# Two state sums moved forward in TensorE's program of a fused attention, scan and gated-product kernel

## What is computed

```python
h = x @ fc1_w.T + fc1_b
xz = h @ in_proj_w.T                      # xc, z = split(xz)
u = silu(conv4(xc) + conv_b)
dt_low, Bm, Cm = split(u @ x_proj_w.T)    # 16 states
dt = softplus(dt_low @ dt_proj_w.T + dt_proj_b)
A = -exp(A_log)
def step(h, t):                           # over 2048 positions
    h = exp(dt_t * A) * h + (dt_t * u_t) * B_t
    y_t = einsum('bdn,bn->bd', h, C_t)
out = (((ys + u * D) * silu(z)) @ out_proj_w.T) @ fc2_w.T + fc2_b
ffn = (silu(x @ w_gate.T / 127) * (x @ w_up.T / 127)) @ w_down.T / 127
x = x + out * silu(ffn)
```

## Time and profile before

| | us |
|---|---|
| median of three runs | 2783.31 |
| lowest and highest run | 2783.25, 2787.44 |
| profiled execution, its own time | 2788.2 |
| its span | 2786.4 |
| PE busy | 2542.0 (91%) |
| DVE busy | 2333.8 (84%) |
| ACT busy | 2011.2 (72%) |
| POOL busy | 2013.2 (72%) |

### The profile page before, as it was taken

The page is one execution under the profiler, slowest core; times in us unless marked ns, Lnnn a source line. Parts: engine busy times, 40 slices in busy tenths (PEclk is TensorE's granted clock), DMA queues, the critical chain, the costliest instruction groups (busy, mean ns, idle before and its releaser), DMA issues. The chain is left out here.

```text
span 2786.4 us, 37406 instructions
## 1 busy us (share of the span) xinstructions
PE 2542.0 (91%) x13454; PEld 1490.8 (54%) x13454; DVE 2333.8 (84%) x2899; ACT 2011.2 (72%) x3253; POOL 2013.2 (72%) x682
## 2 busy tenths in 40 slices
PE   7897899999976799999999999999999999999988
PEld 3454344443443465656656566565655656556565
DVE  7685777777733899898998989989899898998996
ACT  4222466666643798897988979889798897988974
POOL 0656011111211999999999999999999999999996
PEclk9898999999978799999999999999999999999999
DMA  6337999888541231321313213132131321313210
GB/s 188 116 116 179 260 218 236 205 200 224 211 161 49 105 130 29 117 92 46 130 26 119 92 46 130 25 120 92 46 130 24 121 92 46 130 24 114 92 46 8
DMA packets 121586, 316.00 MB, mean 113 GB/s; under 512 B 15517, under 2 KB 76445, under 8 KB 104878
## 3 DMA queue, kind: packets, MB, share of 16 engines
q1 hardware_dynamic: 91210, 233.32, 27.3%
q0 software_dynamic: 27888, 79.24, 10.3%
q10 hardware_dynamic: 2304, 1.05, 0.2%
HBM read 278.89 MB, written 43.13 MB: 116 GB/s over the span
## 5 line engine op out<-in xcount | busy, mean ns | idle before, releaser
L1523 DVE TENSOR_TENSOR_SCAN l_st<-l_p_a,l_hl,l_st 128x512 f32<-128x512 f32 x768 | 930.2, 1263 | 90.5 <-ACT l_p_a L1808 83.3
L1721 POOL TENSOR_TENSOR l_st<-l_st,lw_cs 128x2048 f32<-128x2048 f32 x192 | 878.4, 4634 | 3.2 <-ACT l_hl L1813 3.2
L1808 ACT ACTIVATE l_p_a<-l_dt,lw_a_neg 128x512 f32<-128x512 f32 x1024 | 666.5, 681 | 67.2 <-DVE keep_xg L1523 41.1
L1713 POOL TENSOR_TENSOR l_st<-l_bs,l_dtu 128x2048 f32<-128x2048 f32 (+1 forms) x128 | 555.1, 4337 | 57.2 <-PE l_p_y L2098 53.3
L2098 PEld LDWEIGHTS l_p_y<-keep_ident,l_st 128*128 128x128 f32 x3072 | 355.1, 145 | 118.6 <-issue 73.0
L2098 PE MATMUL l_p_y<-keep_ident,l_st 128*128 128x128 f32 x3072 | 380.5, 281 | 28.7 <-POOL l_st L1721 28.7
L1020 ACT ACTIVATE a_pr<-a_p_s 128x512 f32<-128x512 f32 x512 | 284.7, 596 | 143.8 <-PE a_p_s L1089 140.0
L931 DVE TENSOR_REDUCE a_mpart<-a_p_m 128x1 f32<-128x512 f32 x512 | 312.0, 679 | 12.2 <-PE a_p_m L1045 11.0
L1523 DVE TENSOR_TENSOR_SCAN keep_xg<-l_p_a,l_hl,keep_xg 128x512 f32<-128x512 f32 x256 | 314.5, 1265 | 1.6
L1721 POOL TENSOR_TENSOR keep_xg<-keep_xg,lw_cs 128x2048 f32<-128x2048 f32 x64 | 299.7, 4682 | 2.0 <-ACT l_hl L1813 2.0
L858 POOL DMA_DIRECT2D a_w<-in_w_dram x32 | 23.1, 737 | 327.2 <-PE a_p_m L1119 271.3
(11 more groups left out here) (246 smaller groups left out, 4007.9 us busy)
## 6 DMA issues: line engine op xcount, KB each, us to landing
l_bs<-s_bc SPq DMA_DIRECT2D x64, 1024.0 KB, 4.7
lw_cs<-s_bc SPq DMA_DIRECT2D x64, 1024.0 KB, 4.7
a_w<-in_w_dram POOLq DMA_DIRECT2D x32, 1024.0 KB, 12.0
late<-in_w_dram POOLq DMA_DIRECT2D x32, 1024.0 KB, 19.4
kx<-s_kp SPq DMA_DIRECT2D x96, 256.0 KB, 12.3
s_kp<-late SPq DMA_DIRECT2D x96, 128.0 KB, 2.1
s_vp<-late SPq DMA_DIRECT2D x16, 544.0 KB, 3.5
a_vg<-s_vp SPq DMA_DIRECT2D x16, 544.0 KB, 14.8
```

What stands on the lines that cost most here:

```text
L1523: eng.tensor_tensor_scan(st[k % NG][:, n, :], p_a[:, n, :], st[k % NG][:, n, :], hl[:, k, n:n + 1], ALU.mult, ALU.add).then_inc(scan_ok, 1)
L1713: eng.tensor_tensor(st[n][:, first:NG, :], bs[:, 4 * n + first:4 * n + 4, :], dtu[(k // NG) % 2][:, :].unsqueeze(1).broadcast_to([P, NG - ...
L1721: eng.tensor_tensor(st[n][:, :, :], st[n][:, :, :], cs[:, 4 * n:4 * n + 4, :], ALU.mult).then_inc(cm_ok, 1)
L1808: eng.activation(p_a[:, n, :], dt[c % 2][:, :], ACT.Exp, scale=a_neg[:, c, m:m + 1]).then_inc(dA_ok, 1)
```

## The change

Two calls of `sums` are moved within TensorE's program. No instruction is added or removed, and no other engine's program is changed.

- In the first half of the turn, `step_low(s, 2)` and `sums(s, 1)` stand in front of `mix(f, 0)` instead of behind it. The table `FILLS` is changed to match.
- In the second half, `sums(s, 9)` stands in front of `gate_h(s, 2)` and `up_h(s, 1)` instead of behind them.

```diff
-                 ("op", 0, END, 0), ("dt", 2, SCAN, 1), ("op", 1, END, 1), ("cv", 0, FRONT, 0), ("z", 0, SCAN, 1),
+                 ("dt", 2, SCAN, 1), ("op", 0, END, 0), ("op", 1, END, 1), ("cv", 0, FRONT, 0), ("z", 0, SCAN, 1),
...
                     if scan:
                         sums(s, 0)
+                        step_low(q, s, 2)
+                        sums(s, 1)
                     if end:
                         mix(q, f, p, 0)
                     if scan:
-                        step_low(q, s, 2)
-                        sums(s, 1)
                         sums(s, 2)
                     if end:
                         mix(q, f, p, 1)
...
                     if scan:
+                        sums(s, 9)
                         gate_h(q, s, o, 2)
                         up_h(q, s, o, 1)
-                        sums(s, 9)
```

## The result

The changed kernel has a median of 2806.61 us (four runs, 2805.43 to 2809.04). The kernel before, run beside it, has 2784.86 us (four runs, 2783.25 to 2787.44). The ratio is 1.0078, with a 95% interval of 1.0061 to 1.0096. The change makes the kernel slower by 0.8%. The profiled execution of the changed kernel took 2809.04 us with a span of 2807.2, against 2788.2 and 2786.4 before, so 20.8 us of span are to be explained.

What follows compares the result with a forecast made beforehand. A closed loop of waits through DVE, ACT and TensorE, not POOL, was taken to bound the kernel. 8.4 + 11.2 = +19.6 us, +18.8 with the last turns, gave 2802 us; 8-in-10 range 2789 to 2810.

Steps and rivals of the forecast that it cites:

- The bound: Scan stage: a closed loop of waits through DVE, ACT and TensorE sets the 116.22 us turn, not POOL.
- ring: Closed loop of steps one turn long, each starting because the one before ended; 116.22 us, without POOL.
- Rival A: POOL is the bound after all, so removing its waits makes the kernel faster, 2735 or 2762 us; chance 0.05.
- The slack: POOL's path ends at sums 13; TensorE then still waits 0.22 us for DVE at `up_h` 5.
- First half, worth 0: POOL's 2.00 us wait at slot 5 goes, slot 9 waits about 2.2; bounds -0.1 and +0.1 us a turn.
- `hidden` 1, 14 x 0.6: DVE waits 0.6 us for `up_h` 1, delayed behind the moved sums 9, in 14 turns: +8.4 us.
- The low clock, 7 x 1.6: TensorE's clock falls behind `up_h` 5 in 7 of 14 turns, 1.6 us each: +11.2 us, bounds 0 and 23.
- rival D: Low clock more often: before `gate_h` 3 too, or in nearly all turns at `up_h` 5; 2814 us, chance 0.07.
- Rival B: Only the wait at `hidden` 1 lengthens the turn, the clock stays at 2.4 GHz; 2791 us, chance 0.24.
- The tail, -0.8: In the last turns POOL sets the end and is about 0.8 us sooner, so the end comes earlier.
- The total: Whole kernel: +18.8 us against the median, to 2802 us.

Runs made afterwards that it cites:

- pool_lighter: Kernel before, with POOL's product by C left out for two of the four states of slot 11; 2784.48 us, ratio 0.9996.
- more_pool_2: Changed kernel with two extra unused products on POOL in each turn, behind `dbu` 13; 2804.3 us, ratio 1.0070.
- z_order: Kernel before, with `gate_z` 0 and 1 one block earlier on TensorE and ACT's copy of the first sum later; 2781.94 us, ratio 0.9989.
- first_half: Kernel before with only the first move, `step_low` 2 and sums 1 in front of `mix` 0; 2788.38 us, ratio 1.0007.
- last_old: Changed kernel with sums 9 back at its old place in the last turn alone; 2802.43 us, ratio 1.0063.
- hidden_later: Changed kernel with `hidden` 1 on DVE one scan later, behind scan (12, 0); 2797.09 us, ratio 1.0025.
- second_half: Kernel before with only the second move, sums 9 in front of `gate_h` 2 and `up_h` 1; 2807.0 us, ratio 1.0063.
- more_pool: Changed kernel with one extra unused product on POOL in each turn, behind `dbu` 13; 2805.99 us, ratio 1.0077.

## Why the prediction was right, and where it was not

**The bound.** Right, and shown from both sides: less work on POOL leaves the turn (pool_lighter, 116.21), more leaves it (more_pool_2, 116.77), and a shorter ring shortens it with POOL's waits in place (z_order). Rival A falls for this kernel. It does not fall for z_order, whose ring is 0.5 us shorter and runs over POOL. The slack is less steady than the prediction has it. The 0.22 us at `up_h` 5 are there in the last six of the 14 turns. In the first eight TensorE waits 1.4 us at sums 13 and under 0.1 at `up_h` 5, so the turn that the prediction compares with had just used its slack up.

**First half, worth 0.** Right as the change stood: first_half has the turn of before to 0.01 us, and its 2.00 us came back at slot 9 as 2.31 where about 2.2 was said. In the kernel after, the wait at slot 5 is not wholly gone, 0.43 us in ordinary turns, though it was to be. first_half has no wait there, so it comes with the second half. It cost nothing.

**`hidden` 1, 14 x 0.6.** Right in place and nearly in size. DVE waits 0.46 us there, and the turn grows by 0.57, so 8.0 us for 8.4.

**The low clock, 7 x 1.6.** The mechanism was right, at the forecast place and with the forecast price (1.68 for 1.6). The count was mis-sized: five turns at `up_h` 5 for seven, 8.4 us for 11.2, and 0.7 more in the first turn, of which some 0.5 stand before sums 10, rival D's place. That five came near seven is luck. The share was borrowed from `step_low` 3, and it does not hold even there: the wait of 1.06 us stands in every turn, while the clock is low behind it in eight of 14 turns before, in seven in first_half and in one in the kernel after and in pool_lighter. The wait of 1.5 us in one piece at `up_h` 5 came as 0.21, 0.45 and 0.68, because `up_h` 4 and the 17-row block turned out to have waits of their own as soon as TensorE is early. Rival B, the ring alone, falls for the kernel after, while more_pool_2 shows B's turns but for the low stretches at 47 us.

**The tail, -0.8.** This step failed: +3.8 us. The prediction reasoned that POOL sets the end there and is released sooner. It did not ask what stands behind a sum that itself has to wait for POOL. last_old gives back 2.8 of the 3.8 to 4.6 us. The 0.9 that remain come with the other moved sum, which waits for POOL in the last turn in the same way. What follows the last scan (6, 0) is 0.6 us shorter in last_old than before, near the 0.8 of the prediction. So POOL does set the end there, and what failed is what stands in front of it.

**The total.** +18.8 us was forecast and 20.8 measured in the profiled runs, 21.7 between the medians. The missed 4.6 us of the tail were offset in part by the 2.8 that the clock cost less. The total is nearer than its terms.

## What to carry to other kernels

Find the closed ring of waits before moving anything to feed the busiest engine. Here that engine had waits worth 53 us and not one of them was on the ring. Then ask how much room the paths beside the ring have. Here the busiest engine had 0.6 us, and once the ring was shortened by more, the half of the change that had been worth nothing was worth 0.47 us a turn. When a wait is moved forward on an in-order engine, ask what is queued behind it, and ask again for the first and last turns, where the partner that it waits for runs at another distance. Where a wait is taken away, look where the idle time lands: next to a block with few rows it can cost more than it did.

## What the runs showed of the hardware

- TensorE's clock fell behind waits that are shorter than those that left it alone. 0.45 and 0.68 us on either side of a 17-row block of 1.09 us bring a granted clock of 0.58 over 4 us in five of 14 turns; 1.16 and 0.24 us with 4.7 us of work between them, the same block among it, bring none (more_pool_2). Each low stretch at `up_h` 5 cost 1.68 us of the turn.
- The clock fell at the same place of the program in some turns and not in others. Counting the first turn as 0, they are turns 2, 4, 7, 9 and 11 in the kernel after. With 17 rows and the same 0.45 and 0.68 us in front, it fell in two (pool_lighter), three (hidden_later), four (second_half) and five (last_old, more_pool) of 14. What picks the turn was not found.
- The 128x512 product on POOL with 2-byte output took 1.05 us. Adding two of them to each turn of the engine that is 98% busy in the scan stage did not make the kernel slower (more_pool_2).
